# A dense product for 1536 nodes in the first layer of a graph network, and counting one-hots built by pairs

## The reference

```python
h = relu(layernorm(x))
def sage(h, Wl, bl, Wr):
    agg = segment_sum(h[src], dst, num_segments=12500)
    mean = agg / maximum(deg, 1)[:, None]
    return mean @ Wl + bl + h @ Wr
h = relu(batchnorm(sage(h, Wl0, bl0, Wr0)))    # 128 -> 256
h = relu(batchnorm(sage(h, Wl1, bl1, Wr1)))    # 256 -> 256
out = x + sage(h, Wl2, bl2, Wr2)               # 256 -> 128
```

## Time and profile before

| | us |
|---|---|
| median of 3 runs | 5068.4 (5065.18 to 5078.79) |
| profiled execution, its time | 5089.54 |
| its span | 5087.7 |
| PE, POOL, DVE, ACT busy in it | 3720.6, 3573.8, 2314.3, 697.4 |

### The profile page before, as it was taken

How to read it: one execution, slowest core, us unless ns; L and a number is a source line. 1 busy time by engine, 2 the same in 40 slices (tenths; PEclk the granted TensorE clock), 3 DMA queues, 4 the chain that set the end, 5 groups by cost and what they waited for, 6 DMA issues and landing times.

```text
span 5087.7 us, 70057 instructions
## 1 busy us (share of the span) xinstructions
PE 3720.6 (73%) x16512; PEld 2527.7 (50%) x16512; DVE 2314.3 (45%) x7909; ACT 697.4 (14%) x1817; POOL 3573.8 (70%) x3567
## 2 busy tenths in 40 slices
PE   2446766666666654447899999999988688888776
PEld 1234444444444444446766666666658344444446
DVE  4447767877876667776422222222226122222222
ACT  3001112232233330002300000000002000000002
POOL 2777777777777777772277777777773677777774
PEclk6566666676666565557999999999989788888887
DMA  6112234444444443113667777677766988888886
GB/s 174 47 51 73 97 100 157 162 147 147 163 157 172 175 163 110 48 48 68 227 196 203 204 208 205 200 205 202 203 208 197 245 218 214 216 214 220 207 222 199
DMA packets 781606, 848.84 MB, mean 167 GB/s; under 512 B 69895, under 2 KB 676505, under 8 KB 774394
## 3 DMA queue, kind: packets, MB, share of 16 engines
q1 hardware_dynamic: 654570, 560.41, 36.4%
q0 software_dynamic: 123712, 285.69, 20.0%
q10 hardware_dynamic: 3152, 1.06, 0.1%
HBM read 634.91 MB, written 211.98 MB: 166 GB/s over the span
## 4 chain that ended last, share of the span: by engine, by line
PE 41%; issue 19%; DVE 14%; POOL 11%; DMA 9%; DVEq 4%; SPq 1%; ACT 0%; POOLq 0%; ACTq 0%
PE ps L876 14%; PE ps L1007 13%; POOL ring L650 10%; PE ps L894 6%; DMA ring<-table,idx_now 6%; DVE area L1321 6%; DVE big L1192 2%; PE ps L1034 2%; PE ps L1049 2%; DVEq L1195 1%; DVE area L1167 1%; DVE wrong L1217 1%; DVE area L1220 1%; DVEq L1321 1%; PE ps L902 1%
## 5 line engine op out<-in xcount | busy, mean ns | idle before, releaser
L650 POOL DMA_INDIRECT ring<-table,idx_now x3376 | 3419.6, 1013 | 1175.5 <-issue 1083.1
L876 PEld LDWEIGHTS ps<-onehot,ring 128*128 128x128 f32 x8712 | 1309.8, 230 | 900.3 <-issue 833.3
L876 PE MATMUL ps<-onehot,ring 128*128 128x32 f32 x8712 | 1296.3, 305 | 624.7 <-issue 300.5
L1192 DVE TENSOR_TENSOR big<-big,ps 128x32 f32 (+1 forms) x3376 | 668.0, 198 | 2324.7 <-PE ps L876 1919.6
L1007 PE MATMUL ps<-area 128*128 128x512 f32 (+1 forms) x2744 | 1374.8, 646 | 24.2 <-DMA area<-table 23.3
L894 PE MATMUL ps<-area 128*128 128x392 f16 x2208 | 688.7, 491 | 323.1 <-DVE area L1321 322.7
L1007 PEld LDWEIGHTS ps<-area 128*128 128x128 f32 x2744 | 552.8, 214 | 562.1 <-issue 538.4
L894 PEld LDWEIGHTS ps<-area 128*128 128x128 f16 x2208 | 287.6, 138 | 619.8 <-issue 546.6
L754 ACT ACTIVATE idx_now<-idx_all 128x5 int32 (+3 forms) x716 | 147.5, 207 | 3247.9 <-PE ps L876 3236.6
L1321 DVE TENSOR_SCALAR area<-iota_code,area 128x392 f16<-128x392 f16 x2208 | 570.9, 329 | 0.0
L767 ACT ACTIVATE big<-ps 128x392 f32<-128x392 f32 x736 | 362.0, 498 | 689.8 <-PE ps L894 687.9
(11 more groups left out here) (133 smaller groups left out, 1273.5 us busy)
## 6 DMA issues: line engine op xcount, KB each, us to landing
edge_count<-big SPq DMA_DIRECT2D x46, 3136.0 KB
area<-edge_count SPq DMA_DIRECT2D x98, 1472.0 KB
area<-edge_count SPq DMA_DIRECT2D x98, 960.0 KB, 6.1
ring<-table,idx_now POOLq DMA_INDIRECT x3376
area<-table SPq DMA_DIRECT2D x98, 256.0 KB, 6.7
ring<-input SPq DMA_DIRECT2D x98, 256.0 KB, 2.7
input<-ring SPq DMA_DIRECT2D x48, 512.0 KB, 3.7
area<-table SPq DMA_DIRECT2D x98, 128.0 KB
```

What stands on the lines that cost most here:

```text
L650: pool.indirect_dma_start(out=ring[:, g * n + j, 0:width], out_offset=None, in_=table[layer][:, :], in_offset=bass.IndirectOffsetOnAxis(ap ...
L876: last = nc.tensor.matmul(to[:, m * W:(m + 1) * W], ring[:, k, m * P:(m + 1) * P], onehot[:, k, :], start=True, stop=True)
L1192: V.tensor_tensor(sums, sums, step, ALU.add).then_inc(s_acc[layer], 1)
```

## The change

It gives the first layer a dense product for its first 1536 nodes, so that it gathers only tiles 523 to 1562: 1040 tiles in 52 bodies. The product lies in the last 16 bodies, beside the degrees: one unit to a part, 49 units, so in 12 bodies and one part, in one pass, with four buffers. A unit's counts are 24 half-blocks x 128 words (1536 KB over the 128 partitions) and its rows 128 KB; TensorE does 2 x 3 products of 512 columns with it, into PSUM banks 4 to 6. SP loads the first unit when all counts are stored. At the end ACT copies the three banks to `big`.

The 54 bodies that count become 27 with twice as many steps each (cap 3: 96 to a body, 24 to a part). DVE builds one-hots for up to 8 steps (`LANES`) with two instructions, a low one and a code one, both `tensor_tensor`; the tables `low_all` and `code_all` hold every number twice, as two f16 side by side, and the instructions read them as pairs. TensorE waits once for each such run of steps. The own rows are reloaded after the last unit.

```diff
-DENSE = (0, 30 * HB, HBS * HB)
-FIRST = (0, 583, 747)
+DENSE = (24 * HB, 30 * HB, HBS * HB)
+FIRST = (523, 583, 747)
...
+LANES = 8
...
-SEGMENTS = ((0, 1, 4, 0), (1, 2, 2, 6), (2, 4, 2, 5), (4, 6, 2, 4), (6, 30, 1, 3), (30, 46, 1, 2))
+SEGMENTS = ((0, 1, 2, 0), (1, 2, 1, 6), (2, 4, 1, 5), (4, 6, 1, 4), (6, 30, 0, 3), (30, 46, 0, 2))
...
+        low_all, code_all = (area[:, 2 * STEPS + k * STEP_COLS:2 * STEPS + (k + 1) * STEP_COLS].bitcast(f16)
+                             .rearrange("p (s a) -> p s a", a=2) for k in range(2))
...
-                                counting(range(g * each, (g + 1) * each),
-                                         pair * (2 * GROUPS_HB * cap) + (STEP_BASE[a + half] + g * each * cap),
-                                         pair * 2 + (a + half), half, (cap,) * GROUPS_HB)
-                            body(pair * 2 + (at + half), some)
-                    at += b - a
-            assert 2 * (BODIES[0] - at) == W
-
-            def window_node(i):
-                return lambda g: degrees(i * 2 + (g // 2 - 2 * at), g // 2) if g % 2 == 0 else None
-            body(at, window_node(at))
-            with eng.Fori(at + 1, BODIES[0] - 1) as i:
-                body(i, window_node(i))
-            body(BODIES[0] - 1, window_node(BODIES[0] - 1))
+                        def some(g):
+                            half, first = g // 2, g % 2 * each
+                            counting(range(first, first + each), pair * (2 * GROUPS_HB * cap) + (STEP_BASE[a + half] + first * cap),
+                                     pair * 2 + (a + half), half, (cap,) * GROUPS_HB)
+                        body(pair + at, some)
+                    at += (b - a) // 2
+            assert at == FIRST_TAIL
+
+            def tail_of(i, parts_with_unit):
+                return lambda g: tail(g, i * 2 + (g // 2 - 2 * at) if g % 2 == 0 else None,
+                                      i * PARTS + (g - PARTS * at) if g < parts_with_unit else None, i + (1 - at))
+            body(at, tail_of(at, PARTS))
+            last_units = at + UNITS // PARTS
+            with eng.Fori(at + 1, last_units) as i:
+                body(i, tail_of(i, PARTS))
+            body(last_units, tail_of(last_units, UNITS % PARTS))
+            with eng.Fori(last_units + 1, BODIES[0] - 1) as i:
+                body(i, tail_of(i, 0))
+            body(BODIES[0] - 1, tail_of(BODIES[0] - 1, 0))
...
                 sp.wait_ge(s_count_out[half], 16 * HBS // 2)
+
+            sp.wait_ge(s_count_step, COUNT_STEPS)
+
+            def load_first_unit(b, unit):
+                sp.dma_start(first_counts[b], edge_count.rearrange("h p n -> p h n")[:, 0:DENSE[0] // HB, ds(unit * (2 * HB), 2 * HB)]
+                             ).then_inc(s_unit[b], 16)
+                sp.dma_start(first_rows[b], tb0[:, ds(unit * 2, 2), :]).then_inc(s_unit[b], 16)
+            for b in range(PARTS):
+                load_first_unit(b, b)
+            with sp.Fori(1, UNITS // PARTS) as t:
+                for b in range(PARTS):
+                    sp.wait_ge(s_unit_used, t * PARTS + (b + 1 - PARTS))
+                    load_first_unit(b, t * PARTS + b)
+            for unit in range(UNITS // PARTS * PARTS, UNITS):
+                sp.wait_ge(s_unit_used, unit + 1 - PARTS)
+                load_first_unit(unit % PARTS, unit)
+            sp.wait_ge(s_unit_used, UNITS)
             with if_irregular(sp):
                 sp.wait_ge(s_degree, 1)
...
+            first_bodies(act, body_0, keep_counts, lambda g, w, unit, turn: None)
+            act.wait_ge(s_unit_used, UNITS)
+            act.wait_ge(s_acc[0], BODIES[0] * PER_BODY[0])
+            for b, at in enumerate(range(0, DENSE[0], 512)):
+                wide = min(512, DENSE[0] - at)
+                nc.scalar.activation(big[:, 1, at:at + wide], first_dense_ps(b)[:, 0:wide], ACT.Copy).then_inc(s_dense, 1)
...
                 for k in groups:
                     if not (isinstance(hb, int) and hb == 0 and k < 4):
                         pe.wait_ge(s_count_ev, hb * GROUPS_HB + (k - 3))
                     for c in range(caps[k]):
-                        if n > SLOTS:
-                            pe.wait_ge(s_count_hot, at + 1)
-                            at += 1
+                        if slot == first or slot % LANES == 0:
+                            pe.wait_ge(s_count_hot, step + min(n, slot - first + LANES - slot % LANES))
                         nc.tensor.matmul(ps[:, 4 + k % 4, 0:CODES], low_hot[:, slot % SLOTS, :], code_hot[:, slot % SLOTS, :],
                                          start=(c == 0), stop=(c == caps[k] - 1)).then_inc(s_count_step, 1)
                         slot += 1
...
+            def first_dense(g, unit, turn):
+                if isinstance(unit, int) and unit == 0:
+
+                    pe.wait_ge(s_count_ev, HBS * GROUPS_HB)
+                pe.wait_ge(s_unit[g], turn * 32)
+                for s in range(2):
+                    for b, at in enumerate(range(0, DENSE[0], 512)):
+                        wide = min(512, DENSE[0] - at)
+                        last = nc.tensor.matmul(first_dense_ps(b)[:, 0:wide].rearrange("p (h c) -> p h c", c=HB), first_rows[g][:, s, :],
+                                                first_counts[g][:, at // HB:(at + wide) // HB, s * HB:(s + 1) * HB],
+                                                start=isinstance(unit, int) and unit == 0 and s == 0,
+                                                stop=isinstance(unit, int) and unit == UNITS - 1 and s == 1)
+                last.then_inc(s_unit_used, 1)
+
+            def tail(g, w, unit, turn):
+                if w is not None:
+                    sum_degrees(w, g // 2)
+                if unit is not None:
+                    first_dense(g, unit, turn)
...
+                twice = lambda a: a.rearrange("p (n a) -> p n a", a=1).to_broadcast([P, n, 2])
+                V.tensor_copy(low_all[:, at:at + n, :], twice(ps[:, 5, 0:n]))
                 link(V.tensor_tensor(rel, ps[:, 3, 0:n], bound_row[:, at:at + n], ALU.subtract))
...
+                link(V.tensor_scalar(code_all[:, at:at + n, :], twice(rel), 1.0, None, ALU.subtract))
...
                 while done < n:
                     at = (slot + done) % SLOTS
-                    count = min(n - done, SLOTS - at)
+                    count = min(n - done, LANES - at % LANES)
                     if not isinstance(step, int) or step + done + count > SLOTS:
                         dve.wait_ge(s_count_step, step + (done + count - SLOTS))
-                    one_hots(low_hot[:, at:at + count, :], iota_code[:, 0:P], low_all[:, ds(step + done, count)])
-                    for c in range(count):
-                        V.tensor_scalar(code_hot[:, at + c, :], iota_code[:, :], code_all[:, ds(step + (done + c), 1)], None,
-                                        ALU.is_equal).then_inc(s_count_hot, 1)
+                    for hots, w, values in ((low_hot, P, low_all), (code_hot, CODES, code_all)):
+
+                        shape = [P, count, w // 2, 2]
+                        ins = V.tensor_tensor(hots[:, at:at + count, :].rearrange("p s (n a) -> p s n a", a=2),
+                                              iota_code[:, 0:w].rearrange("p (b n a) -> p b n a", b=1, a=2).to_broadcast(shape),
+                                              values[:, ds(step + done, count), :].rearrange("p s (b a) -> p s b a", b=1).to_broadcast(shape),
+                                              ALU.is_equal)
+                    ins.then_inc(s_count_hot, count)
                     done += count
...
                 dve.wait_ge(s_h0T_out[u], 16 * uses(CHUNKS, u, DEPTH))
-            first_bodies(dve, body_0, count_hots, window_degrees)
+            first_bodies(dve, body_0, count_hots, lambda g, w, unit, turn: window_degrees(w, g // 2) if w is not None else None)
+            dve.wait_ge(s_dense, dense_kept(0))
             dve.wait_ge(s_acc[0], BODIES[0] * PER_BODY[0])
-
-            link(V.tensor_scalar(degrees[0:BLOCKS, :], degree_ps, 1.0, None, ALU.max))
             dve.sem_inc(s_degree, 1)
-            V.reciprocal(degrees[0:BLOCKS, :], degrees[0:BLOCKS, :]).then_inc(s_inv, 1)
-
             with if_irregular(dve):
                 for half in range(2):
                     dve.wait_ge(s_count_out[half], 16 * HBS // 2)
@@ -1369,8 +1446,11 @@
                 V.tensor_copy(bucket_no, iota_row[:, 0:BUCKETS])
                 V.memset(counts, 0.0)
```

More of the change, by code:

```diff
@@ L73 @@
 TABLE_BODIES = 9
-assert len(STEP_CHUNKS) == 5 and TABLE_BODIES + sum((b - a) * n for a, b, n, _ in SEGMENTS) < BODIES[0]
+FIRST_TAIL = TABLE_BODIES + sum((b - a) * n if n else (b - a) // 2 for a, b, n, _ in SEGMENTS)
+FIRST_UNIT_WORDS = 2 * DENSE[0] + 2 * IN_C
+assert len(STEP_CHUNKS) == 5 and 2 * (BODIES[0] - FIRST_TAIL) == W and UNITS // PARTS < BODIES[0] - FIRST_TAIL - 1
 assert all(b == 2 * TURN + 1 for b in BODIES[1:2]) and BODIES[2] > 2 * TURN + 1
@@ L288, in gnn_kernel @@
```

(28 more changed lines are left out.)

61 lines of the change are left out of this document (33 added, 28 removed).

## The result

The changed kernel takes 4706.0 us in the median of four runs (4702.9 to 4709.2), against 5069.3 for the one before in the same session (5065.2 to 5078.8): a ratio of 0.928 [0.9265, 0.9297]; brackets give the 95% interval of a ratio. The forecast was 4560 us, range 4450 to 4780: the sign and the range held, the value is 146 us short. The profiled run took 4704.5 us with a span of 4702.6.

A forecast was written before the change was run, and what follows sets the result against it. The prediction took POOL and DVE together to bound the first layer. Untouched 3122.5 + counting 910 + tail 537 + small edits 9 = 4578.5 us, 4560 after allowing for the profiled run's 21 over its median; range 4450 to 4780.

The forecast's parts named there:

- 27 bodies fewer: First layer: 52 bodies in place of 79, 27 of them counting; 764 us to be had at the old pace.
- Blocks of 2.5 us: Counting stretch: DVE makes the one-hots of eight steps in 2.5 us, pairs running at half of L1167's time per element.
- rival A: Counting one-hots: pairs run at the plain rate, block 4.68 us, stretch 1500, total 5147 us, slower; chance 0.08.
- POOL: 27 x 25.0 = 675: Counting stretch: POOL needs 675 us at 25.0 us a body, gathers at 0.95 us, so it runs ahead of DVE.
- DVE's chain in cap-3 bodies: Counting stretch: DVE sets the pace, 690 us of blocks plus 183 of adds and hots, 910 us with 4% for waits.
- rival C: Counting stretch: count stores starve the gathers, 6.98 us for each of 46 stores, +320, total 4880 us; chance 0.09.
- The tail: Last 16 bodies: loads set 34.2 us a body with units, TensorE 31 just under; 537 us against 438, between 480 and 620.
- Dense work now fills all but some 1.5 us: Tail: dense work covers TensorE's 5.8 us wait for DVE's degree hots, twice a body, except for some 1.5 us.
- rival B: Tail: it serialises with TensorE at 1.2 GHz, 58 us a body, tail 829, total 4850 us; chance 0.11.
- the signs that were to show the forecast's tail: Tail windows: DMA share 0.9 or more, TensorE waiting for loads, granted clock above 0.8, POOL waiting for indices.
- The DMA price: Tail: a unit's load takes 6.7 us, a body 31.5 us if DMA never idles, 34.2 at 0.92 busy.
- Rival D: Tail: it hides its loads and stays at 27.4 us a body, total 4459 us; chance 0.12.

The follow-up runs named there:

- the second experiment: Kernel after the change, with the code one-hots made one step at a time by tensor_scalar and the low ones still by pairs: 4742.6 us, 0.934.
- the swap: Kernel after the change, with the unit's product put before the degree product on TensorE in each part of the tail: 4569.6 us, 0.900.

## Why the forecast was right and where it was wrong

Of the 146 us, 85 lie in the counting stretch, 57 in the tail, -16 in the rest, and 20 in that the run of after is 1.6 us under its median where the one of before was 21 over its own (the forecast's rounding takes 2 back). The sign was safe with 27 bodies fewer. The range held because it was wide and not because its steps were right: both stretches came out long, each for a reason that the prediction does not have.

**27 bodies fewer: right.** 541 gathers stand in the stretch in place of 1080, and everything from 1964 us on took what it did, but for 8 us.

**Blocks of 2.5 us: right**, measured 2.47. With single values the same instructions take 3.42 + 1.22 = 4.64 us, rival A's 4.68, and the kernel is slower than before (rival A said 5147 us, it is 5196). So A's price of a block was sound, and its condition was false. Its stretch of 1500 us came out as 1496; the 49 us more are mostly the tail's, which is priced at 537 in A too and takes 594 in the kernel after. The Trainium skill (VectorE: DVE Perf Modes, The perf-mode tier table) gives such an operation twice the plain rate: 3419 over 1785 ns is 1.92, with the fixed part in both.

**"POOL: 27 x 25.0 = 675", and that POOL "now runs ahead": the step that failed first.** It rests on gathers of 0.95 us "since L1321 is gone"; measured are 1.476. The 1.91 us gather of the earlier trace rows starts at 1548.07, inside L1167's compare (1547.93 + 1.22 = 1549.15), and ends 0.83 us after it. I put it down to the code one-hots, yet it was the compare beside it that held it. A code one-hot holds a gather too (the one that starts 0.08 us into it ends 0.82 us after it), but it is only 0.33 us long: 307 gathers that start in an L1321 take 947 ns in the median and 1036 in the mean. What counts is how long an instruction that holds lasts, and not that it has two operands, as the 1664-element `tensor_scalar` above shows; the change made one instruction of 1.785 us out of eight short ones. In the cap-2 bodies a gather takes 1447 ns and a gap 0.29 us, so 20 of them 34.8 us, against 32.6 measured: POOL enters these bodies with a lead and has only 150 gathers to do in them, not 160. That is the 38 us missed in the eight cap-2 bodies (the terms give 223 for them): POOL is busy 217.1 of 261 us and idle before its gathers for the rest, 43.9 of it their gaps. The stores' register loads alone would have cost nearly as much there, 29.7 us in the second experiment.

```profile
L699 POOL DMA_INDIRECT ring<-table,idx_now x150 | 217.1, 1447 | 47.1 <-issue 43.9 <-ACT idx_now L803 3.2
```

**DVE's chain in cap-3 bodies: right in its terms, one missing.** A part is 3 x 2.47 + 1.69 = 9.10 us, 36.4 a body, with the 4% 37.9. Measured 41.0, and 38.6 when the stores come in quarters (with POOL as the bound). The missing term is DVE's register loads beside a store, 4.4 us in each of 12 bodies, 53 us; the 4% for waits covered 18 of them, and 492 against the 459 of the terms are the 33 missed. The prediction costed the stores against the gathers alone (rival C). For the other 14 us, in the first seven bodies, the cause is open.

**The tail: right sum of parts, wrong order.** "Dense work now fills all but some 1.5 us" of the degree wait: measured 3.6 to 3.95 us, since the degree hots are made only after the part's adds and hots, and the degree product stands ahead of the dense one on TensorE. The wait costs twice: itself (2 x 3.8 = 7.6 us a body), and the lower clock behind it (0.8 to 1.6 us on the unit, 0.7 on the degree product, so 2 x 1.9 = 3.8). Together that is 11.4 us, and the swap took 11.1 of a body behind the first. So the chain is 27.6 + 7.6 + 3.8 = 39.0 us (39.1 measured), not 31, and the loads, which I took for the bound at 34.2, are hidden: leaving them out changes nothing. This is rival B in a mild form (0.84 and not 0.50), and neither it nor the forecast named the order as the lever. Of the signs that were to show the forecast's tail, TensorE waiting for loads and a DMA share of 0.9 did not come: it waits for them once, 10.9 us in the first body, and the share is 0.82. The start is priced right: that body is 12.7 us longer than the others, against 15.

**The DMA price: too high.** 31.5 us was to be the body's time "if the DMA engines never idle"; with the product first it is 28.0 behind the first body while they never do. The shares of the earlier trace rows were taken as engine time; with the product first the two queues' shares add up to 1.16, so packets overlap and such a share overstates the engine time.

**Rival C: its mechanism is there in small.** In the cap-2 bodies of the kernel after, TensorE waits 72.5 us before its gather products, in 13 waits of at most 6.6 us for 16 stores. But DVE, which waits for the sums, idles 40.9 us there, and POOL has no time left over, so the stores' own share on the path isn't told apart; it is nowhere near the 6.98 us a store over the whole stretch. **Rival D** (27.4 us a body) was wrong for this kernel, but the swapped one comes within 0.6 us of it behind its first body (28.0).

## What the runs showed of the hardware

**A held gather.** An indirect DMA issued by POOL that starts while DVE runs a `tensor_tensor` with both operands in SBUF ends 0.82 us after it, at the plain rate (3.42 us, gather 4.16) and at the double one (1.79, gather 2.0). So do 20 of 30 that start in a `tensor_scalar` of 1664 elements (1.08 us, gather 1.53). Beside the adds, which read one operand from PSUM, and beside a reduction of 1.88 us it takes 0.95. The Trainium skill (SBUF — State Buffer, SBUF: two separate sides) says that VectorE and GpSimd share a port pair by an exclusive lock, which a VectorE instruction takes in a two-port mode, or with two SBUF inputs against GpSimd work that reads SBUF. The rows agree for the compares, with 0.82 us from their end to the gather's. For the `tensor_scalar` the mode is not in the rows; its 1.08 us for 1664 elements are 0.65 ns an element, near the double rate of the compares (1785 ns for 3136, 0.57).

**A register load beside a store.** 0.6 us at the least, up to 4.8 where the stores are of 3136 KB, not over 2.4 where they come in quarters.

**A clock lost to short waits.** After TensorE waited 3.6 to 3.95 us, 13 degree products took 1.62 us instead of 0.89, the lower of its two levels, and the 12 half products behind them up to 1.6 us more than 5.4. After waits of 0.3 to 0.7 us nothing was lost (12 half products in 5.42 us).

Open remain the stalls at fixed places in DVE's loop with single one-hots (up to 2.6 and 3.1 us, 22 in 12 bodies); no run took them apart.

## What to carry to other kernels

Fewer and larger VectorE instructions are not free for the engine beside it: before merging, look in the trace at which gathers are long and which instruction they start in, and choose the form by which engine is the bound in that stretch (here, beside stores in quarters, single ones with cap 2 were 47 us better than pairs; with cap 3 pairs were better while the stores were whole, and beside quarters single ones were not tried there). Where TensorE must wait for a late producer, put work that is ready ahead of it: this one swap gave 136 us, the wait and the clock. And cost a large store not only against the loads, but also against the small reads that steer an engine.
